# A graph layer over 32 batches on one core: the work ahead of the loop shared out anew between VectorE and GpSimd

## What is computed

```python
h = jnp.maximum(_layernorm(x, axis=-1), 0.0)
q = jnp.einsum('c,bcn->bn', wq, h)
k = jnp.einsum('c,bcn->bn', wk, h)
scores = q[:, None, :] + k[:, :, None]
scores = jnp.where(scores > 0, scores, NEG_SLOPE * scores)
att = jax.nn.softmax(scores, axis=-1)
agg = jnp.einsum('bcn,bmn->bcm', h, att)
out = jnp.einsum('oc,bcm->bom', wm, agg) + bm[None, :, None]
return x + jax.nn.relu(out)          # wm is the input adj
```

## Time and profile before

| | us |
|---|---|
| median of 3 runs | 2090.09 |
| lowest and highest | 2087.72, 2090.14 |
| the profiled execution, whole | 2090.47 |
| its span, first to last instruction | 2088.7 |
| TensorE busy | 2051.5 |
| VectorE busy | 1674.8 |
| GpSimd busy | 379.6 |

### The profile page before, as it was taken

How to read it: one execution, slowest core, us unless ns; L and a number is a source line. 1 busy time by engine, 2 the same in 40 slices (tenths; PEclk the granted TensorE clock), 3 DMA queues, 4 the chain that set the end, 5 groups by cost and what they waited for, 6 DMA issues and landing times.

```text
span 2088.7 us, 33534 instructions
## 1 busy us (share of the span) xinstructions
PE 2051.5 (98%) x10448; PEld 950.3 (45%) x10448; DVE 1674.8 (80%) x3661; ACT 1221.5 (58%) x1871; POOL 379.6 (18%) x273
## 2 busy tenths in 40 slices
PE   5899999999999999999999999999999999999999
PEld 2344444444444444444444444444444444444444
DVE  7978878778887788887788877888877888778853
ACT  5556656556655566565566555665655665556634
POOL 1012211112111122111121111221111211112212
PEclk9999999999999999999999999999999999999999
DMA  5244433344324444333433234442334432343332
GB/s 195 64 155 142 148 99 123 138 160 141 133 84 136 151 141 146 104 118 137 161 141 133 84 136 151 141 146 105 117 137 161 141 131 86 136 152 141 106 101 76
DMA packets 126395, 271.46 MB, mean 130 GB/s; under 512 B 22624, under 2 KB 23136, under 8 KB 122208
## 3 DMA queue, kind: packets, MB, share of 16 engines
q1 hardware_dynamic: 123904, 269.01, 37.1%
q10 hardware_dynamic: 2400, 1.58, 0.3%
HBM read 202.91 MB, written 67.63 MB: 130 GB/s over the span
## 4 chain that ended last, share of the span: by engine, by line
PE 95%; DVE 3%; DMA 1%; POOL 0%; issue 0%; ACT 0%; POOLq 0%; SPq 0%; DVEq 0%
PE mix L385 21%; PE mix L387 21%; PE mix L386 21%; PE mix L362 10%; PE mix L363 10%; PE mix L364 10%; PE small L325 2%; DVE den_out L728 1%; PE small L334 1%; DMA xs<-in_x_dram 0%; DVE p_ring L749 0%; DVE p_lo L756 0%; DVE v_lo L761 0%; POOL wm_nat L893 0%; DMA den_row<-den_rows 0%
## 5 line engine op out<-in xcount | busy, mean ns | idle before, releaser
L385 PE MATMUL mix<-p_hi,v_hi 128*128 128x512 f16 x2048 | 776.3, 379 | 5.9 <-DVE p_lo L756 5.4
L386 PE MATMUL mix<-p_lo,v_hi 128*128 128x512 f16 x2048 | 776.2, 379 | 0.0
L387 PE MATMUL mix<-p_hi,v_lo 128*128 128x512 f16 x2048 | 776.2, 379 | 0.0
L911 POOL TENSOR_TENSOR res<-res,y 128x512 f32<-128x512 f32 x256 | 370.5, 1447 | 1688.2 <-ACT y L512 1688.2
L749 DVE SCALAR_TENSOR_TENSOR p_ring<-ab_row,cols,p_ring 128x512 f32<-128x512 f32 x512 | 377.1, 748 | 129.7 <-ACT p_ring L491 129.7
L491 ACT ACTIVATE p_ring<-ab_row,cols 128x512 f32<-128x512 f32 x512 | 349.5, 691 | 192.4 <-DMA ab_row<-ab_rows 132.3
L503 ACT ACTIVATE v_hi<-mix 128x512 f16<-128x512 f32 x256 | 152.7, 597 | 444.1 <-PE mix L364 443.5
L728 DVE SCALAR_TENSOR_TENSOR den_out<-den_row,cols 128x512 f32<-128x512 f32 x512 | 393.4, 806 | 1.0 <-DMA den_row<-den_rows 1.0
L362 PE MATMUL mix<-wmT_hi,h_hi 128*128 128x512 f16 x1024 | 389.1, 380 | 0.0
L364 PE MATMUL mix<-wmT_hi,h_lo 128*128 128x512 f16 x1024 | 388.8, 380 | 0.0
L363 PE MATMUL mix<-wmT_lo,h_hi 128*128 128x512 f16 x1024 | 388.8, 380 | 0.0
(11 more groups left out here) (71 smaller groups left out, 838.9 us busy)
## 6 DMA issues: line engine op xcount, KB each, us to landing
res<-in_x_dram SPq DMA_DIRECT2D x256, 256.0 KB, 3.2
out_dram<-res SPq DMA_DIRECT2D x256, 256.0 KB, 2.1
xs<-in_x_dram SPq DMA_DIRECT2D x124, 512.0 KB, 6.5
den_row<-den_rows SPq DMA_DIRECT2D x32, 1024.0 KB, 4.6
ab_row<-ab_rows SPq DMA_DIRECT2D x64, 512.0 KB, 5.0
res<-in_x_dram SPq DMA_DIRECT2D x4, 512.0 KB, 5.0
wm_nat<-in_adj_dram ACTq DMA_DIRECT2D x1, 1024.0 KB, 12.2
den_rows<-cols SPq DMA_DIRECT2D x32, 8.0 KB, 1.6
```

The source lines that it names most:

```text
L385: pe.matmul(ps[:, :], v_hi[:, b[1], nt, chans], p_hi[:, hf, nt, :], start=(nt == 0), stop=False)
L386: pe.matmul(ps[:, :], v_hi[:, b[1], nt, chans], p_lo[:, hf, nt, :], start=False, stop=False)
L387: mm = pe.matmul(ps[:, :], v_lo[:, b[1], nt, chans], p_hi[:, hf, nt, :], start=False, stop=(nt == NT - 1))
L911: pool.tensor_tensor(res[:, k, :], res[:, k, :], y[:, k % 2, :], ALU.add).then_inc(s_add, 1)
```

## The change

1. VectorE makes `weight_scales` right after the first batch's normaliser, ahead of `h_full_first`, and then scales the first two tiles of `wm_nat` itself. GpSimd scales the other two. Each half has a semaphore.
2. GpSimd scales and splits the weights of q and k (four small operations in a chain), after its two tiles of `wm_nat` and ahead of the select weights.
3. GpSimd makes h_lo of the second batch, four tiles of 128x1024. It is L910 of the changed kernel; VectorE's four `h_lower(second, ct)` are gone.
4. VectorE takes all four statistics of the second batch ahead of `q_tail(first)`, where before there were two ahead and two behind.
5. With h_lo gone, tiles 0 and 1 of `denominator(first, ...)` stand together. The others alternate with `v_lower`. Tile 5 moves from behind `q_rows(second)` to ahead of `v_lower(first, 7)`.
6. `v_lower(second, 0)` stands ahead of `q_tail(second)`, and `copy_ab(first)` right behind it, ahead of all statistics of the third batch.

DEN_PARTS stays 2: a tile of denominators is still two instructions.

```diff
             for ct in range(CT):
                 statistics(first, ct)
             normaliser(first)
+            weight_scales()
+            for ot in range(2):
+                dve.tensor_scalar(wm_nat[:, ot, :], wm_nat[:, ot, :], inv2[:, ot:ot + 1], V_BITS,
+                                  ALU.mult, ALU.mult).then_inc(s_wm[0], 1)
             h_full_first(0)
             h_full_first(1)
-            weight_scales()
-            h_lower_first(0)
-            h_lower_first(1)
-            scaled_wqk()
-            h_lower_first(2)
-            h_lower_first(3)
+            for ct in range(CT):
+                h_lower_first(ct)
...
             pool.wait_ge(s_su, 3)
-            for ot in range(OT):
+            for ot in range(2, OT):
                 pool.tensor_scalar(wm_nat[:, ot, :], wm_nat[:, ot, :], inv2[:, ot:ot + 1], V_BITS,
-                                   ALU.mult, ALU.mult).then_inc(s_wm, 1)
+                                   ALU.mult, ALU.mult).then_inc(s_wm[1], 1)
+            pool.wait_ge(s_wv, 16 * 3)
+            for i in range(2):
+                pool.tensor_scalar(wqk_col[:, i, :], wqk_col[:, i, :], inv2[:, OT + i:OT + i + 1], Q_BITS,
+                                   ALU.mult, ALU.mult).then_inc(s_wc, 1)
+            pool.wait_ge(s_wc, 3)
+            hi = wqk[:, :, 0:4].rearrange("p t (i s) -> p s i t", s=2)
+            pool.tensor_copy(hi[:, 0], wqk_col[:, :, :]).then_inc(s_wc, 1)
+            pool.wait_ge(s_wc, 4)
+            pool.tensor_tensor(hi[:, 1], wqk_col[:, :, :], hi[:, 0], ALU.subtract).then_inc(s_wqk, 1)
...
+            for ct in range(CT):
+                pool.wait_ge(s_hhi, CT + ct + 1)
+                pool.wait_ge(s_h32, CT + ct + 1)
+                pool.tensor_tensor(h_lo[:, 1, ct, :], h32[:, ct % 2, :], h_hi[:, 1, ct, :],
+                                   ALU.subtract).then_inc(s_hlo, 1)
```

More of the change, by code:

```diff
@@ L146, in gnn_layer @@
         s_su = sem("scaling_chain")
-        s_wz = sem("wqk_zeroed")
+        s_wc = sem("wqk_chain")
         s_un = sem("unscales_ready")
@@ L150, in gnn_layer @@
         s_wqk = sem("wqk_ready")
-        s_wm = sem("wm_scaled")
+        s_wm = [sem(f"wm_scaled_{i}") for i in range(2)]
         s_wt = sem("wmT_transposed")
@@ L307, in transposed_weights @@
                 for ot in range(OT):
[L308 removed]
+                    pe.wait_ge(s_wm[ot // 2], ot % 2 + 1)
                     for ct in range(CT):
@@ L825, in _ @@
             q_head(first)
-            statistics(second, 0)
-            statistics(second, 1)
+            for ct in range(CT):
+                statistics(second, ct)
             q_tail(first)
-            statistics(second, 2)
-            statistics(second, 3)
             normaliser(second)
@@ L835, in _ @@
             denominator(first, 0)
-            for ct in range(CT):
-                h_lower(second, ct)
-                v_lower(first, 3 + ct)
-                denominator(first, 1 + ct)
+            denominator(first, 1)
+            v_lower(first, 3)
+            denominator(first, 2)
+            v_lower(first, 4)
+            denominator(first, 3)
+            v_lower(first, 5)
+            denominator(first, 4)
+            v_lower(first, 6)
+            denominator(first, 5)
             v_lower(first, 7)
             q_rows(second)
-            denominator(first, 5)
             denominator(first, 6)
@@ L846, in _ @@
             row_scales(first)
+            v_lower(second, 0)
             q_tail(second)
-            v_lower(second, 0)
+            copy_ab(first)
             v_lower(second, 1)
             statistics((1, 0), 0)
+            statistics((1, 0), 1)
             v_lower(second, 2)
-            statistics((1, 0), 1)
-            copy_ab(first)
+            statistics((1, 0), 2)
             v_lower(second, 3)
-            statistics((1, 0), 2)
             statistics((1, 0), 3)
```

15 lines of the change are left out of this document (2 added, 13 removed).

## The result

The changed kernel took 2093.0 us (median of 19 runs, 2090.02 to 2093.63), the kernel before on the same chip 2088.59 (19 runs, 2087.29 to 2090.14). The ratio is 1.0021, 95% interval 1.0014 to 1.0027. This is a small loss of 4.4 us; its interval reaches from 2.9 to 5.6 us and excludes zero. The prediction was 2091.9, with a range of 2087.0 to 2095.0.

A forecast was written before the change was run, and what follows sets the result against it. The prediction took TensorE, busy 98% of the span, as the bound, with VectorE's stream setting its last p_lo. Terms 1.3 - 4.5 + 4.8 + 1.0 - 0.8 = +1.8 us on 2090.09 gave 2091.9, range 2087.0 to 2095.0.

The forecast's parts named there:

- The frame: Whole span: TensorE is full, so a change ahead of the loop is worth what it moves the last p_lo.
- first denominator: VectorE's first denominator, behind GpSimd's h_lo 0: starts at 45.6, not 44.26, +1.3 us; `den_row` there at about 44.5.
- four h_lo off VectorE: VectorE's stream in the second batch: four h_lo of 1.13 us leave it, -4.5 us.
- blocks: VectorE's denominators behind the first: three waits for GpSimd's h_lo, 1.6 us each, +4.8 us.
- waits for TensorE (maximum, `copy_ab`): VectorE at `copy_ab(first)`: arrives at 66.8, waits for the transposition of ab until 67.6, +1.0 us.
- the 0.76 us at `weight` gone: VectorE ahead of the first `weight`: `ab_row` arrives ahead of need, so this idle time goes, -0.8 us.
- The start: Ahead of the first projection: q and k weights ready at 26.6, projection at about 26.7, 0.3 us earlier.
- my third rival: Start: GpSimd's small operations get in between VectorE's, projection at 25, chain 1.5 to 2 us earlier; 2084 to 2086, chance 0.08.
- The price of h_lo: GpSimd, second batch: each h_lo taken as 2.35 us, bounds 1.27 and 2.54.
- Where GpSimd gets in: GpSimd's h_lo beside VectorE's denominators: never run together; GpSimd enters each time VectorE turns from denominators to v_lo.
- The clock: TensorE ahead of the second projection: about 4.6 us idle drops the clock, +1.4 to +3.0 us more, 2093.3 to 2094.9; chance 0.25.

The follow-up runs named there:

- e12: e7 plus constant matmuls on TensorE, 58 ahead of the weights' transposes and 12 behind; 2085.49 us, ratio 0.9985 to the kernel before.
- e7: The kernel before with only the start of the change (weight scaling split between VectorE and GpSimd, q and k weights on GpSimd); 2089.34 us, ratio 0.9998.
- e5: The changed kernel with GpSimd's second-batch h_lo over 512 columns, not 1024, the rest zero; 2087.77 us, ratio 0.9995 to the kernel before.
- e13: The changed kernel with 12 matmuls on the weights in TensorE's 2.92 us wait ahead of the second batch's selection; 2090.59 us, ratio 1.0012 to the kernel before.
- e11: The changed kernel plus constant matmuls on TensorE, 58 ahead of the weights' transposes and 12 behind; 2088.07 us, ratio 1.0000 to the kernel before.
- e10: The kernel before with 72 constant matmuls on TensorE ahead of the weights' transposes; 2087.55 us, ratio 0.9995 to the kernel before.
- e2: The kernel before with only h_lo of the second batch moved from VectorE to GpSimd; 2088.29 us, ratio 1.0006 to the kernel before.
- e3: The changed kernel with `copy_ab(first)` moved back behind three v_lo; 2091.24 us, ratio 1.0014 to the kernel before.

## Why the prediction was right, and where it was not

The frame held. TensorE is full, its last wait for p_lo moved by +1.82 us, and the profiled time by +1.96 (2090.47 to 2092.43). The waits for p_lo kept their sum of 5.4 us. The steps, each against what the rows show:

| step | predicted | in the profiles |
|---|---|---|
| first denominator | +1.3 | -1.9 (44.26 to 42.34) |
| four h_lo off VectorE | -4.5 | -4.5 |
| blocks | three of 1.6 = +4.8 | four: 1.24 + 1.86 + 1.86 + 1.24 = +6.2 |
| waits for TensorE (maximum, `copy_ab`) | +1.0 | 0.82 + 1.88 = +2.7 |
| the 0.76 us at `weight` gone | -0.8 | -0.8 |
| sum | +1.8 | +1.7 |

So the sum was right in part by luck: one term was 3.2 us too high and two together 3.1 us too low. Of the +1.3 forecast for the first denominator 1.1 us were h_lo 0 in its way, so the blocks as a whole were forecast well (5.9 for 6.2). What failed is the time at which den_row comes, +0.2 for -1.9, and the waits for TensorE, +1.0 for +2.7.

*The start.* I had GpSimd's first weight tile end at 22.8 and its small operations wait until VectorE's run ended at 25.5. Both weight tiles ran from 17.22 in 1.83 us, so the transposes were over at 21.4 and not at 27.1 as before; the small operations got in between VectorE's instructions and ended at 23.83 and not at 26.6. (Before, VectorE had them done at 23.2; what held the projection then was the last weight tile.) The projection now waited for VectorE's last h_lo, which ended at 24.89. This is the mechanism of my third rival, to which I gave 0.08. Its other half, that the 2 us reach the end, is seen in e12: with the constant matmuls they are worth 2.1 us. Without them e7 shows nothing clear of noise.

*The price of h_lo.* 2.35 us was too long; it is 2.13.

*Where GpSimd gets in.* I had it come in only where VectorE turns from denominators to v_lo. It came in wherever it was ready. At 42.34 and 50.61 the half came upon an h_lo already running (1.99 us). At 44.93 and 47.47 (2.61 us) the h_lo had become ready during the half ahead and went first, once between two tiles and once between the two halves of one. With 2.13 us each VectorE paid 4.5 + 1.7. That the two engines don't share held for every denominator half beside an h_lo: the Trainium skill's "SBUF - State Buffer", section "SBUF: two separate sides", states this, and 2.61 us for a half of 0.74 agrees with it; e5 shows that the block follows the length.

*The clock.* I gave 0.25 to a fall behind a stretch of 4.6 us ahead of the second projection. The place was wrong: h_lo was ready at 52.06, the projection started at 53.44 and not at 57.8, and v tile 7 waited, 1.77 us, for v_lo. The stretch was the one ahead of the selection, where I had put half a us: 2.92 us, since `q_rows(second)` ended near 60 and v tile 0 some 3 us ahead of it. Behind it the clock fell, and e13 prices that at 1.6 us (rows) to 2.4 (median). So the clock rival happened along with my forecast, and 1.6 us of VectorE's waits for TensorE (2.70 less the 1.12 of e13) are its mark. The Trainium skill's "TensorE: Matmul & The Clock Gate", section "Why this matters for your kernels", warns of this; the 0.43 us behind 60.11 agree. The length of the wait alone doesn't tell, though: in e11 one of 2.91 us at the same place left the clock up, as one of 2.78 us had ahead of the second projection in before, while 2.64 us there in e7 and 2.05 us in e10 brought it down. So the place that my rival named is exposed as well.

*Why the medians say 4.4.* The forecast took the median of before from three runs at 2090.09, and the profiled execution lay at 2090.47. Over the four sets of runs of before the median is 2088.3 to 2089.0 and the range 2086.1 to 2090.4. The profile of before lay 1.9 us above its median (2088.59) and that of the changed kernel 0.6 below its own; with the 1.96 us between the profiles that makes the 4.4. In the profile of before the clock rose only at 34.5, and VectorE stood 1.85 us at the first maximum. e2 has the start of before, its profiled execution rose at 29.5, the maximum ran at 32.69 without a wait, and e10's constant matmuls bring the median to 2087.6. I took one late rise to be the kernel's. The changed kernel is exposed in two places, at the first v tiles and at the selection, and lies between 2092.1 and 2093.6 in 18 of 19 runs.

What the clock and the order do, from four medians:

| | before | start alone | whole change |
|---|---|---|---|
| as it stands | 2088.3 to 2089.0 | 2089.3 (e7) | 2093.0 |
| with constant matmuls at the start | 2087.6 (e10) | 2085.5 (e12) | 2088.1 (e11) |

With the constant matmuls the start gains 2.1 us and the rest of the change loses 2.6, which is about e11's blocks (5.9 - 4.5) and its wait of 1.12 us at `copy_ab`. Without them no gain of the start is seen and the whole loses 4.4 (4.0 to 4.7 against the other sets). What decides when the clock first rises in a given execution stays open: among the profiles with the changed start and without the constant matmuls it lay at 31.4 to 34.5.

## What to carry to other kernels

Before you move an elementwise operation from VectorE to GpSimd, compare its length there with its length here: if VectorE works from SBUF at that time it will stand for nearly all of it, once for each instruction, and 2.13 us for 1.13 is a loss. Ahead of a loop, where TensorE has gaps, look at the distance of its matmuls in more than one profile; one line that makes TensorE wait 3 us (here `q_rows` behind two tiles too many) can cost the lower clock behind the wait on top, 1.6 us here. Matmuls on a constant in the time that it waits anyway brought 3.9 us (e12 against e7) and 4.9 us (e11); in the kernel before the 1.5 us of e10 are not clear of noise. A sum against a single profile takes over whatever that execution happened to do, so ask for the spread of the runs first.

## What the hardware did that I had not expected

- The clock's first rise moved by 5 us between executions of kernels with the same start (29.5 in e2, 34.5 in before), and the runs of before spread over 4 us. With the constant matmuls the 11 runs of a kernel spread over 1.4 to 3.2 us.
- Behind a wait of 2.92 us the clock was down for 7 matmuls in the changed kernel and for 12 in e3; behind one of 2.05 us in e10 it fell too, and behind one of 2.91 us in e11 it didn't.
- GpSimd got in between two back-to-back denominator halves of VectorE when it was ready in time (2.61 us for 0.74), but before it had waited out two h_lo in a row (2.77 us). Operations of 4 to 8 elements that take 0.2 us alone took 1.06 to 1.68 us beside VectorE's h_lo.
- The write of 8 KB of exponentials took 1.6 to 3.1 us, longer in the profiles in which the clock rose late.
